# Second attention of a two-layer network: head pairs in row halves, causal mask on GpSimd, row maxima per pair, one batch after the other

## The reference, cut to what matters

```
qkv = x @ w_attn + b_attn                 # 256 -> 768
q, k, v = heads of 16 features each       # 16 heads
att = (q @ k.T) / 4
att = where(tril, att, -inf)              # causal: key <= query
att = softmax(att, axis=-1)
y = (att @ v), heads side by side         # 1024 x 256 in each batch
return y @ w_proj + b_proj
```

## Time and profile before

| | |
|---|---|
| times shown | 2521.11, 2525.0, 2533.97 us |
| span of the profiled execution | 2511.1 us (13.9 us below the median of the times) |
| instructions in the span | 38834 |
| PE busy | 2345.1 us (93%) |
| DVE busy | 1599.4 us (64%) |
| ACT busy | 1220.8 us (49%) |
| POOL busy | 497.4 us (20%) |
| second attention, prologue | 1523 to 1605 us |
| second attention, steps with scores | 1605 to 2131 us |
| its tail | 2131 to 2147 us |

### The profile page before, as it was taken

The page is one execution under the profiler, slowest core; times in us unless marked ns, Lnnn a source line. Parts: engine busy times, 40 slices in busy tenths (PEclk is TensorE's granted clock), DMA queues, the critical chain, the costliest instruction groups (busy, mean ns, idle before and its releaser), DMA issues. The chain is left out here.

```text
span 2511.1 us, 38834 instructions
## 1 busy us (share of the span) xinstructions
PE 2345.1 (93%) x12832; PEld 1844.3 (73%) x12832; DVE 1599.4 (64%) x2872; ACT 1220.8 (49%) x2202; POOL 497.4 (20%) x416
## 2 busy tenths in 40 slices
PE   5999999999999999999998795999999999799996
PEld 4887888878888888888886683555555555788885
DVE  5676667666766666667677565545555555476665
ACT  4565555545655555456555435245555455333333
POOL 4021020120210201202110236001111112233323
PEclk9999999999999999999999895869999899699998
DMA  2010010100100101001000101000000000000001
GB/s 73 1 37 2 1 37 2 37 2 1 37 2 1 37 2 37 2 1 37 17 1 11 41 7 36 1 3 1 3 0 1 0 1 1 26 20 25 25 19 34
DMA packets 35542, 38.86 MB, mean 15 GB/s; under 512 B 6928, under 2 KB 31760, under 8 KB 35344
## 3 DMA queue, kind: packets, MB, share of 16 engines
q1 hardware_dynamic: 35344, 36.43, 5.2%
HBM read 34.32 MB, written 2.10 MB: 15 GB/s over the span
## 5 line engine op out<-in xcount | busy, mean ns | idle before, releaser
L758 DVE TENSOR_REDUCE attn_neg_max<-psum 128x1 f32<-128x1024 f32 x256 | 313.3, 1224 | 200.4 <-PE psum L93 171.9
L716 ACT ACTIVATE attn_probT_hi<-psum 128x512 fp32r<-128x512 f32 x512 | 278.1, 596 | 298.9 <-PE psum L602 298.9
L804 DVE TENSOR_TENSOR attn_probT_lo<-psum,attn_probT_hi 128x512 fp32r<-128x512 f32 x512 | 327.6, 682 | 28.3 <-ACT attn_probT_hi L716 27.9
L1637 DVE TENSOR_REDUCE attn_peaks<-psum 128x1 f32<-128x512 f32 (+3 forms) x384 | 211.8, 557 | 191.7 <-PE psum L1438 95.1
L695 ACT ACTIVATE attn_prob<-psum,attn_neg_max 128x1024 f32<-128x1024 f32 x256 | 286.7, 1120 | 23.4 <-DVE attn_neg_max L758 23.4
L602 PE MATMUL psum<-ident_sb,attn_prob 128*128 128x128 f32 x2048 | 266.5, 273 | 33.1 <-ACT attn_prob L695 24.3
L1578 ACT ACTIVATE attn_probT<-psum 128x512 f32<-128x512 f32 (+3 forms) x384 | 181.7, 491 | 235.9 <-PE psum L1469 168.8
L602 PEld LDWEIGHTS psum<-ident_sb,attn_prob 128*128 128x128 f32 x2048 | 235.8, 140 | 75.9 <-DVE attn_probT_lo L804 27.3
L533 POOL TENSOR_TENSOR attn_v_lo<-x_sb,attn_v_hi 128x512 fp32r<-128x512 f32 x64 | 82.1, 1284 | 778.9 <-ACT attn_v_hi L724 778.9
L93 PE MATMUL psum<-attn_probT_hi,attn_v_hi 128*128 128x512 f32 x512 | 211.5, 413 | 0.6 <-DVE attn_probT_lo L804 0.6
L93 PE MATMUL psum<-attn_probT_lo,attn_v_hi 128*128 128x512 f32 x512 | 201.1, 393 | 0.0
(11 more groups left out here) (203 smaller groups left out, 5278.2 us busy)
## 6 DMA issues: line engine op xcount, KB each, us to landing
moe_staged<-in_moe_w SPq DMA_DIRECT2D x18, 384.0 KB, 3.1
mlp_staged<-in_ffn_w SPq DMA_DIRECT2D x6, 384.0 KB, 3.4
acc_sb<-in_x SPq DMA_DIRECT2D x4, 512.0 KB, 5.6
x_sb<-in_wq_codes SPq DMA_DIRECT2D x8, 256.0 KB, 2.6
x_sb<-in_wq_scales SPq DMA_DIRECT2D x32, 64.0 KB, 3.3
x_sb<-in_wk_codes SPq DMA_DIRECT2D x8, 256.0 KB, 3.7
x_sb<-in_wk_scales SPq DMA_DIRECT2D x32, 64.0 KB, 3.4
x_sb<-in_wv_codes SPq DMA_DIRECT2D x8, 256.0 KB, 3.7
```

What stands on the lines that cost most here:

```text
L716: nc.scalar.activation(probT[0][:, g % 2, half_tile * GT:(half_tile + 1) * GT, j * P:(j + 1) * P], ring(use).rearrange("p (t n) -> p t n", ...
L758: nc.vector.tensor_reduce(neg_max[:, i % 2:i % 2 + 1], scores(i), AX.XY, ALU.max, negate=True).then_inc(max_ready, 1)
L804: nc.vector.tensor_tensor(to[1], ring(use).rearrange("p (t n) -> p t n", n=P), f32(to[0]), ALU.subtract).then_inc(ring_free, 1)
L1637: nc.vector.tensor_reduce(peaks[:, half % 2, n % HALF:n % HALF + 1], max_bank(n)[:, 0:width], AX.X, ALU.max, negate=True).then_inc(max_fre ...
```

## The change

- **Halves.** The order is now all four passes of batch 0, then of batch 1. The engine loop is gone: all is unrolled, and semaphore counts are constants. A step is now a (chunk, key tile) with all four heads, a quad: 12 to a half, 96 in all.
- **Tiles.** q and key are kept per pair of heads (two heads in one 128-row tile, 64 rows each). ScalarE copies a pair in one instruction; the rows of ones in key come from that instruction's bias, so nothing is cleared beforehand.
- **Scores.** A head's scores are a matmul over its own 64 rows; the two of a pair follow each other and go to different banks. There is no mask matmul: GpSimd clears the entries above the diagonal after the exponential (`hide_later`, `affine_select`), two instructions on each of the 8 diagonal quads of a half, and `weigh_v` waits for them there.
- **Maxima.** A unit is (chunk, query tile, key part) with four heads. The two heads of a pair fill the two banks, and the next pair waits until both banks have been reduced. Units of 128 or 256 keys hold both pairs in the two banks, and one instruction reduces two heads. The mask is now two matmuls over 64 rows for each head instead of one over 128.
- **Shift.** The maxima are turned by four matmuls per pair that also put them into the right rows, and VectorE adds the whole 128-row result to q: two instructions per chunk instead of four.
- **Small work.** `small_work` fixes it by quad. v of batch 1 is projected during halves 2 and 3. The sums are spread with a transpose.

Cut to its core:

```diff
-    half_steps = [(c, kt, h) for c in range(chunks) for kt in range((c + 1) * GT) for h in range(HG)]
-    LEAD_SCORES, LEAD_MAX, FIRST = 3, 40, 16
-    SCORE_BANKS, PROBS = 3, 6
+    quads = [(c, kt) for c in range(chunks) for kt in range((c + 1) * GT)]
+    units = [(c, t, part) for c in range(chunks) for t in range(c * GT, (c + 1) * GT) for part in range(c + 1)]
+    LEAD, FIRST, TAIL = 10, 13, 10
+    SCORE_BANKS, PROBS = 3, 8
+    unit_packed = lambda u: 2 * unit_width(u) <= NB
+    unit_fills = lambda u: 2 if unit_packed(u) else 4
+    small_work = {
+        0: [("stack", 1, 0, 0), ("stack", 1, 0, 1)],
+        1: [("stack", 1, 0, 2), ("stack", 1, 0, 3), ("sums", -1, 1, 0)],
+        2: [("shift", 0, 1, 0), ("shift", 0, 1, 1)],
+        3: [("project", 1, 1, 0), ("spread", -1, 1, 0)],
+        4: [("stack", 1, 1, 0), ("stack", 1, 1, 1)],
+        5: [("stack", 1, 1, 2), ("stack", 1, 1, 3), ("sums", 0, 0, 0)],
+        6: [("out", -1, 1, 0)],
+        7: [("out", -1, 1, 1), ("spread", 0, 0, 0)],
+        8: [("shift", 1, 0, 0), ("shift", 1, 0, 1)],
+        10: [("out", 0, 0, 0)],
+        11: [("out", 0, 0, 1), ("project", 2, 0, 0)],
+    }
...
+            def hide_later(g):
+                c, kt = quads[g % QUADS]
+                if kt < c * GT:
+                    return
+                q0 = queries_from(c, kt)
+                for pair in range(pairs):
+                    pool.wait_ge(exp_done, g * HG + 2 * pair + 2)
+                    at = probT[:, slot(g, 2 * pair):slot(g, 2 * pair) + 2, q0:q0 + P]
+                    nc.gpsimd.affine_select(out=at, in_=at, pattern=[[0, 2], [1, P]], compare_op=ALU.is_ge, fill=0.0,
+                                            base=0, channel_multiplier=-1).then_inc(masked, 1)
...
-                mm = nc.tensor.matmul(bank, q[b][h][rows, t * P:(t + 1) * P], key[b][h][rows, keys], start=True, stop=not own)
-                if own:
-                    mm = nc.tensor.matmul(bank[:, -P:], ident_b[:], masks[:, 0, :], start=False, stop=True)
+                if fill >= 2:
+                    pe.wait_ge(max_free, fill)
+                for i, pair in enumerate(range(pairs) if unit_packed(u) else (pair_of_fills,)):
+                    to = [max_bank(fill + n)[:, i * width:(i + 1) * width] for n in range(2)]
+                    for n in range(2):
+                        mm = nc.tensor.matmul(to[n], q[half % 2][pair][rows(n), t * P:(t + 1) * P],
+                                              key[half % 2][pair][rows(n), keys], start=True, stop=not unit_masked(u))
+                    if unit_masked(u):
+                        for part_of_mask in range(2):
+                            for n in range(2):
+                                mm = nc.tensor.matmul(to[n][:, width - P:width], ident_half[rows(n), part_of_mask, :],
+                                                      mask[rows(n), part_of_mask, :], start=False, stop=part_of_mask == 1)
...
-                mm = nc.tensor.matmul(score_bank(g)[:, q0:], key[b][h][:, kt * P:(kt + 1) * P],
-                                      q[b][h][:, c * NB + q0:(c + 1) * NB], start=True, stop=kt < c * GT)
-                if kt >= c * GT:
-                    mm = nc.tensor.matmul(score_bank(g)[:, q0:q0 + P], ident_b[:], masks[:, 1, :], start=False, stop=True)
+                for h in (2 * pair, 2 * pair + 1):
+                    n = g * HG + h
+                    if n >= SCORE_BANKS:
+                        pe.wait_ge(exp_done, n - SCORE_BANKS + 1)
+                    nc.tensor.matmul(score_bank(n)[:, q0:], key[half % 2][pair][rows(h), kt * P:(kt + 1) * P],
+                                     q[half % 2][pair][rows(h), c * NB + q0:(c + 1) * NB],
+                                     start=True, stop=True).then_inc(scores_full, 1)
...
+                if diagonal[g % QUADS]:
+                    pe.wait_ge(masked, pairs * (half * diagonals_before[-1] + diagonals_before[g % QUADS] + 1))
...
+            def step(g):
+                for pair in range(pairs):
+                    if 0 <= g + 1 < TOTAL:
+                        scores(g + 1, pair)
+                    if 0 <= g + LEAD < TOTAL:
+                        maxima(g + LEAD, pair)
+                    if pair == 0 and 0 <= g < TOTAL:
+                        weigh_v(g)
+                small(g)
...
-                nc.vector.tensor_reduce(peaks[:, half % 2, n % HALF:n % HALF + 1], max_bank(n)[:, 0:width], AX.X, ALU.max,
-                                        negate=True).then_inc(max_free, 1)
+                for n in range(unit_fills(u)):
+                    dve.wait_ge(max_full, fill + n + 1)
+                    if unit_packed(u):
+                        nc.vector.tensor_reduce(to[:, n:HG:2], max_bank(fill + n)[:, 0:2 * width].rearrange("p (i k) -> p i k", i=2),
+                                                AX.X, ALU.max, negate=True).then_inc(max_free, 1)
```

More of the change, by code:

```diff
@@ new lines, in attention1_stage @@
+    unit_fills = lambda u: 2 if unit_packed(u) else 4
+    fills_before = list(itertools.accumulate((unit_fills(u) for u in units), initial=0))
+    HALF_FILLS = fills_before[-1]
+    diagonal = [kt >= c * GT for c, kt in quads]
+    diagonals_before = list(itertools.accumulate(diagonal, initial=0))
+    small_work = {
[11 more added lines that the diff above has]
+    }
@@ new lines, in step @@
+            def step(g):
+                if 0 <= g + 1 < TOTAL:
+                    hide_later(g + 1)
+                half, r = g // QUADS, g % QUADS
+                if r == 9 and 0 <= half + 1 < HALVES:
+                    take_v(half + 1)
+                if r == 6 and 0 <= half + 2 < HALVES:
+                    split_weights(half + 2)
+                for (c, quad), n in Y_AFTER.items():
+                    of = half - c
+                    if r == quad and 0 <= of < HALVES:
+                        make_y(of, c, n)
+                for kind, of, c, n in jobs(g):
@@ L1398, in step @@
-                    if kind == "spread":
-                        out_operand(m, half, c, first_use[g] + n)
                 if g in NORM_ACC_POOL:
@@ L1473, in project_qk @@
-            def project_qk(m, half, c, bank):
-                pe.wait_ge(w_ready, m + half // BATCH + 1)
-                tokens = slice(half % BATCH * SEQ + c * NB, half % BATCH * SEQ + (c + 1) * NB)
-                return project(nc, bank, lambda kt: [x[:, kt, :] for x in w], lambda kt: [x[:, kt, tokens] for x in k.xT])
-            def stack(m, half, j, bank):
-                c, pair, which = stack_jobs[j]
-                pe.wait_ge(qk_lo, m * BATCH * chunks + half * chunks + c + 1)
-                for part in range(2):
-                    mm = nc.tensor.matmul(bank, to_stack[:, (which * pairs + pair) * 2 + part, :], qk[part][:, c, :],
-                                          start=part == 0, stop=part == 1)
-                return mm
@@ new lines, in scores @@
+            def scores(g, pair):
+                half, (c, kt) = g // QUADS, quads[g % QUADS]
+                q0 = queries_from(c, kt)
+                if kt == 0:
+                    pe.wait_ge(shifted, (half * chunks + c) * pairs + pair + 1)
+                for h in (2 * pair, 2 * pair + 1):
[5 more added lines that the diff above has]
+                                     start=True, stop=True).then_inc(scores_full, 1)
@@ new lines, in step @@
+                        if which:
+                            nc.scalar.activation(key[of % 2][pair][:, chunk(c)], misc_bank(use), ACT.Identity,
+                                                 bias=ones_key[:, 0:1]).then_inc(stacked, 1)
+                        else:
+                            nc.scalar.activation(q[of % 2][pair][:, chunk(c)], misc_bank(use), ACT.Copy).then_inc(stacked, 1)
+                        act.wait_ge(stacked, (of * chunks + c) * 2 * pairs + part + 1)
+                        act.nop().then_inc(misc_free[use % 2], 1)
@@ L1649, in take_shift @@
+            def take_shift(half, c, fills):
+                of_chunk = peaks[:, half % 2, unit_start[c]:unit_start[c + 1], :]
+                by_pair = lambda a: a.rearrange("p t (pair i) -> p t pair i", i=2)
+                hi, lo = (shift[:].rearrange("p pair t (i n) -> p t pair i n", i=2)[:, :, :, :, SHIFT_ROW + n] for n in range(2))
+                dve.wait_ge(max_free, fills)
                 if c == 0:
-                    nc.vector.tensor_copy(by_head(peak[:]), of_chunk[:, :, :, :, 0]).then_inc(peak_done, 1)
+                    of_tile = of_chunk
@@ L1723, in step @@
                     after.add_up(dve, NORM_X_DVE.index(g))
+            places = [(first_use[g] + n, job) for g in sorted(first_use) for n, job in enumerate(jobs(g))]
+            shift_uses = [use for use, (kind, of, c, part) in places if (kind, part) == ("shift", pairs - 1)]
+            batch_done = next(use for use, job in places if job == ("out", passes - 1, chunks - 1, 1))
             before.rest_of_acc(dve)
```

625 lines of the change are left out of this document (278 added, 347 removed).

## The result

The changed kernel takes 2392.65 us (median of 4 runs, 2390.32 to 2396.61), the kernel before 2524.53 on the same chip: a ratio of 0.9486, interval 0.9451 to 0.952. It is faster by 132 us. The forecast was 2430, a gain of 95, so 37 us of the gain were not foreseen. The profiled execution of the changed kernel has a span of 2392.5 us and a time of 2394.22.

The account below looks back on a forecast made before the run. PE in its order was taken as the bound before, the ring of two maxima banks after. Loop -83, prologue -15 and clearing +3 make -95 us on a span of 2511.1, so 2416; plus 13.9 gives 2430 us, range 2365 to 2525.

Parts of the forecast that it names:

- the likeliest case: Whole kernel: the forecast of 2430 us, with its own range of 2400 to 2465 and chance 0.49.
- The pair overlaps: PE: a pair's two 64-row matmuls run beside each other in the array's halves; without overlap up to 0.21 us more each.
- The drains: PE: about 0.18 us of each 0.42 goes at a change between matmuls over 128 and 64 rows, two per step before.
- The ring of two maxima banks: Each fill waits for DVE's reductions of both banks: 38 us a half, 51 with small work and longer quads.
- The clock: PE in the loop: 25% of the time at 1.2 GHz, at 84 us a half, making a half 57 us.
- The last half: Last half of the loop: its last ten quads have no maxima, stacks or projections, -15 us.
- What lies around the span: Outside the profiled span: 13.9 us between span and median of the times, carried over from the kernel before.
- Prologue and clearing: Prologue before the first scores: -15 us; GpSimd's clearing above the diagonal: 0.61 us each, +3 us in all.
- No overlap: Rival, PE: the pair does not overlap, a half takes 64 us instead of 57; 2485 us, chance 0.13.
- The clock holds: Rival, PE: only 2% of the time at 1.2 GHz, a half of 52 us; 2390 us, chance 0.14.
- Slow clearing: Rival, GpSimd: 1.35 us per clearing makes `weigh_v` 1.2 us late in 64 diagonal quads, +75; 2505 us, chance 0.08.
- slower by a low clock: Rival, PE: waits for DVE's ring keep three quarters of the stage at 1.2 GHz; 2560 us, chance 0.12.

Follow-up runs that it names:

- experiment 1: Changed kernel with both heads of a pair reading array rows 0 to 63 in scores and maxima, so no overlap within a pair: 2515.67 us, ratio 0.9985.
- Experiments 8 and 9: Changed kernel with both heads' scores on array rows 0 to 63 (8), or scores over all 128 rows (9): 2408.42 and 2398.74 us.
- experiments 3 and 4: Changed kernel with maxima reductions (3), or exponentials from the seventh quad on (4), over half their columns: 2356.7 and 2386.64 us.
- experiments 3 and 10: Changed kernel with maxima reductions over half their columns (3), and with exponentials over half as well (10): 2356.7 and 2354.37 us.
- experiment 6: Changed kernel with one wait for each maxima bank instead of one for both: 2382.05 us, ratio 0.948.
- experiment 2: Changed kernel without the clearing above the diagonal; GpSimd waits and signals without selecting: 2381.91 us, ratio 0.9462.
- experiment 11: Changed kernel with a wait for each maxima bank, the mask by matmul and the output bank's copy moved up in ACT's queue: 2376.13 us, ratio 0.9446.

## Why the prediction was right, and where its sizes were off

The mechanism held and the time lies in the range; the likeliest case's own range (2400 to 2465) missed it by 7 us. Where the 37 us are:

| term | forecast | measured | difference |
|---|---|---|---|
| what is added to the span | 13.9 | 0.15 | -14 |
| seven halves at 2.4 GHz, without v | 7 x 51.3 = 359 | 7 x 48.9 = 342 | -17 |
| v of batch 1 | +3 | 2 x 2.7 = 5 | +2 |
| 1.2 GHz in the seven halves | 39 | 18 | -21 |
| last half | 57 - 15 = 42 | 48.4 | +6 |
| prologue, with the stages ahead | -15 | -11 + 3 | +7 |
| clearing | +3 | 0 | -3 |

The 39 are 7 x (56.9 - 51.3); the seven halves measured 366 us together, and 366 - 342 - 5 leaves 18. The differences add up to -40, of which 2 are rounding, and the seams of the cuts give the last 1: the loop is 415 us from score to score and 414.3 by halves, and what follows it 0.4 longer.

- **The pair overlaps.** Right. Without it nothing of the gain is left (experiment 1). At full clock it is worth 7 us a half, which is half of the way from 64 to 49; the other 8 come from the grouping and the masks that went.
- **The drains.** The 0.18 us a change was not tested alone, and the rows after bear it out only in part. In the quad shown, 0.33 us pass from the pair of scores to the pair of maxima, with no change of rows between them, and 0.33 from there to `weigh_v`, with one. Equal matmuls of 512 columns follow each other at 0.23 to 0.24 (1709.00, 1709.24), and from the last of them to a pair of scores, a change from 128 rows to 64, it takes 0.32 (1709.56). So about 0.1 goes between two pairs with no change at all, a change to 64 rows cost 0.1 here, and one to 128 rows behind a pair 0 or 0.1 more than the pair's own (0.33 to `weigh_v`, 0.42 from 1733.78 to 1734.20). Experiments 8 and 9 have the same number of changes and cannot price them. The group of four came out at 0.66 and 0.88 us where 0.75 was forecast, so the sum held though its parts did not.
- **The ring of two maxima banks.** Right in kind: 2.1 us a turn against 1.87 and 2.01, and experiments 3 and 4 tell the reductions from the exponentials. The half that was built on it, 51.3 us at 2.4 GHz, was 2.4 too long: it measured 48.9. Which of its small terms was too large is open. PE's own work, put at 46 us a half, was right: experiments 3 and 10 end at 46.2 and 45.8. So the ring had some 3 us above it and not 5, which is why relieving it gave 28 us and not 40. DVE was said to be PE's longest wait, and it is ACT. And the hand-over is worth less in the ring than its 12 us (experiment 6).
- **The clock.** This is the step that was most off in size, and it is the share, not the price. A quarter of the time at 1.2 GHz at 84 us a half was taken. The price came out at 82. The share in the first seven halves was 0.14, and with 48.9 and 82 that makes 18 us where 0.25 would have made 39. The 0.25 was a choice between bounds that no row could settle.
- **The last half.** It lost its maxima and its projections, but ran at 1.2 GHz for 0.59 of its length (PEclk 0.71), so it came out at 48.4 and not 42.
- **What lies around the span.** The 13.9 us were carried from the kernel before as if fixed. The kernel before ranges from 2499.89 to 2538.57 over all its runs, and an execution of the changed kernel is 1.7 us longer than its span (2394.22 against 2392.5). So the profiled execution of before was a short one, and the 13.9 were spread, not a part of the time.
- **Prologue and clearing.** The prologue fell by 11 to the 15 forecast. The select took 0.41 us, below the 0.61 taken, and costs nothing that can be told (experiment 2).
- **The output copy** was only in the sum of quad 4, not as something that `weigh_v` waits for. PE waits 29 us for it in all, and by experiment 11 little of that is time.
- **The rivals.** No overlap: did not come. When made true it measured 2516 and not 2485: its 7 us a half held, but half of the loop fell to 1.2 GHz and not a quarter. The clock holds (2390): the nearest number, by luck, since 19% of the loop was at 1.2 GHz and not 2%; what its halves of 52 us and its 13.9 had too much is about what the clock and the last half cost. Slow clearing and slower by a low clock: neither. The Trainium skill, page "Perfetto Trace Analysis", section Matmul Optimizations, says that the matmul engine "dynamically scales power based on utilization". Taken as a rule for the granted clock, with PE's busy share as the utilization, the runs do not agree: PE busy for 99% of the loop had 16% of it at 1.2 GHz before, 90% had 19% after, and 97% had half in experiment 1; filler in PE's gaps left the last half at 0.49. The Trainium skill, page "TensorEngine Tiling (Array Packing)", section Theoretical Speedup, says up to 2x at 64 rows. The trace agrees for the pair itself (0.49 us for one or two scores); to what follows it is less, 0.33 us a pair against 2 x 0.23 for two equal matmuls, so 1.4x.

## What to carry to other kernels

Two matmuls over 64 rows, in different halves of the array and into different banks, run at the same time when they follow each other without a wait: put what pairs side by side in the queue, and first of all those that stand inside a hand-over between engines. The longest wait in the profile is not the bound: halve each suspect once, and believe the one that moves the time. When the ring is 3 us of 49 above PE's own work, relieving it gives that and no more. Compare only stretches with the same work in them, and take the clock out first: halves of 49, 51 and 56 us here are one program, with or without v and with more or less of 1.2 GHz. And before you add what lies between a span and a median, ask how widely the executions spread.

## What was not expected of the hardware

- Without overlap in the pairs the clock stood at 1.2 GHz for 0.50 of the loop, with it for 0.19, at the same columns in all. The kernel before, also without overlap, had 0.16. What decides it is open; PE's busy share does not, and filler did not in the one trial.
- Within one group the kernel before spread over 31 us (13 runs, 2507.14 to 2538.57) and experiment 1 over 30 (10 runs, 2498.94 to 2528.76), the changed kernel over 7 (4 runs, 2379.4 to 2386.59). The mean granted clock of each execution goes with it: in the 13 runs the shortest had 0.947 and the longest 0.934, with a correlation of -0.92, and about 20 us for each 0.01 of clock. That is what the price above gives: 0.01 of mean clock is 2% of the time, 50 us, at 1.2 GHz, and of 50 us at 82 a half instead of 48.9 some 20 are lost (an estimate).
- A select on GpSimd over 128 partitions and 256 elements took 407 to 425 ns, a third of the 1278 ns of a TENSOR_TENSOR with two inputs of 512 elements (L1343).
- The causal mask as matmuls on PE, 512 more of them in the loop, cost 0.8 us a half at full clock and nothing in the time that can be told.
